# Attention with an image prompt: the Gram sum in 9 matmuls a group, its last one behind the product with V

## The chip, the cores and the metric

The kernel runs on one core of a Trainium2 chip. The metric is the device time of one execution in microseconds: 407.49 as the median of three runs (407.61, 407.49 and 405.20).

## The reference

For each of 8 batches there are 112 queries of 320 channels (20 heads of 16) and a context of 375 tokens of 512 channels, the last 4 of which are an image prompt. Besides the ordinary attention over the 371 text tokens, each head needs the norm of the probability-weighted mean of the raw context.

```python
scores_t = einsum('bhsd,bhtd->bhst', q, k_t) * attn_scale
probs_t  = softmax(scores_t)
text_out = einsum('bhst,bhtd->bhsd', probs_t, v_t)
qsem = l2norm(einsum('bhst,bte->bhse', probs_t, text_ehs))
sem  = einsum('bhse,bne->bhsn', qsem, l2norm(ip_ehs))
fused = einsum(q, k_ip) * attn_scale + 0.5 * sem
probs_ip = softmax(fused) * spatial_mask
out = (text_out + probs_ip @ v_ip) @ W_out + b_out + hidden_states
```

## The kernel before

**The Gram form.** The norm of qsem is not formed from its 512 channels. With G = X X^T over the tokens (371 x 371) and e the exponentials of one head and query, the squared norm is e^T G e. G is cut into three row blocks of 128, 128 and 115 tokens. Only the blocks on and above the diagonal are kept; those above it are counted twice (scale 2.0 in lines 683 and 824). Each block is held as two fp32r parts: Gh is rounded by ACT, Gl is the remainder, made by DVE from the same PSUM bank.

**Units and the order.** `master_schedule` writes out one order of units by hand; every engine walks through it and does its part of each unit, so the order is that of TensorE, and a wait on any engine holds what stands behind it there. `behind` changes the order for DVE alone. A batch has five groups of four heads (words in ROUNDS, one string a group; EARLY is batch 0, SECOND the first group of batch 1, LATE the last group of batches 5 and 6, LAST batch 7). While the groups of batch b run, the units of batch b+1 and the K units of batch b+2 are woven in. The words are:

- St (S0, S1, S2): scores of the next group for a third of the tokens, four matmuls; ACT makes the exponentials `big` (line 703) and a rounded copy `er` (line 707).
- gram (g2, g1, g0, or g for all three): Y = sum over the blocks i up to j of G(i,j)^T e(i), 6, 4 and 2 matmuls of 448 columns (lines 1070 to 1074). DVE multiplies Y by e(j) (line 852), POOL adds the three products (line 565). Y has two PSUM banks, so g0 waits for the product of g2.
- v (pv): the product with V for the group before, and the sums, into O; ACT copies O to OT (line 715).
- G0, G1, G2: the row blocks of G of the next batch, 12 matmuls each of 376, 248 and 120 columns. K0, K1, K2 and V0, V1, V2: the keys and values. m (max): a plain score matmul of one head of the next batch, whose row maximum DVE takes (line 830); there are 20 in a batch. mT: the transpose of the maxima, whose result goes by DMA to qst.
- T0, T1: transposes of OT (line 1105), copied by ACT to R (line 722); r0, r1, r2, pw, z and p are the small steps on POOL, DVE and ACT that make the image-prompt probabilities; pT transposes these (line 1110), cT and o make the output.
- E, El: the rounding split of the context of a batch, by ACT (line 652) and by DVE (line 770, batches 0 and 1) or POOL (line 570).

**The ring.** The units K, G, V, T, pT, cT, o, max and mT take three PSUM banks PR in strict turn: a unit waits until the unit three places before it in the ring has been read out (`freed`). The queries' and keys' terms go through DRAM: ks is written to kd and loaded into kst by DMAs of SP (lines 443 and 376).

In the prologue the order is: split of batch 0, queries, K of batch 0, image-prompt keys and values, split of batch 1, G of batch 0, K of batch 1, then the three V of batch 0 and the qip units spread among the 20 max units of batch 0, mT, G of batch 1, St of group 0 with K0 of batch 2.

## Time and profile before

| what | value |
|---|---|
| runs | 407.61, 407.49, 405.20 us, median 407.49 |
| profiled execution | 406.79 us, of it the span 404.6 us |
| PE busy | 391.4 us (97%), 3680 matmuls |
| PEld busy | 323.8 us (80%) |
| DVE, ACT, POOL busy | 223.1 (55%), 205.2 (51%), 208.1 us (51%) |
| chain that ended last | 86% PE; Y 26%, PR 42%, P 9%, O 8% |
| Gram matmuls | 480, in two groups of 95.3 and 87.3 us busy |
| DMA | 38.03 MB, mean 94 GB/s |

PE is TensorE's matmuls and PEld its weight loads, which run beside them. A record of a matmul is longer than the time until the next one may start, so busy times of PE overlap; the steps between starts tell the cost. In the trace all matmuls have the line of a helper, 947, and the PSUM tile tells them apart: Y is the Gram, P the scores, O the product with V, PR the ring. In brackets behind a row stands how long the engine was idle before it and what ended that.

### The profile page before, as it was taken

The numbers are of one execution on the slowest core, as the hardware profiler recorded it, in microseconds if no ns is written. First come the engines' busy times: TensorE is split into PE (matmuls) and PEld (weight loads), VectorE is DVE, ScalarE is ACT, GpSimd is POOL, SyncE is SP. The second block draws the span as 40 slices with busy tenths as digits, with TensorE's granted clock in tenths as the row PEclk, the third lists the DMA queues.
The fourth block names the chain that finished last, engine by engine and source line by source line (L and its number), as shares of the span: only waits on it lengthen the run. The fifth ranks groups of instructions, "written<-read, shape, count | busy, mean of one in ns | idle before, by whom it ended". The sixth has DMA issues, their size and how long they took to land.

```text
span 404.6 us, 9573 instructions
## 1 busy us (share of the span) xinstructions
PE 391.4 (97%) x3680; PEld 323.8 (80%) x3680; DVE 223.1 (55%) x502; ACT 205.2 (51%) x486; POOL 208.1 (51%) x220
## 2 busy tenths in 40 slices
PE   8999998999999999999999999999999999999985
PEld 6548888778788888888889888888888878886763
DVE  0798363675466535665465636653476547644433
ACT  1434234564646564546456554556454466457822
POOL 3020271282537772586437652787258433935972
PEclk9999999999999999999999999999999999999999
DMA  8499986347204802372217420470208110000000
GB/s 268 125 285 235 217 162 127 102 150 135 70 2 151 147 13 73 107 154 39 83 36 187 75 69 17 151 147 16 72 15 181 29 40 2 2 14 30 2 16 15
DMA packets 29455, 38.03 MB, mean 94 GB/s; under 512 B 14361, under 2 KB 26745, under 8 KB 28729
## 3 DMA queue, kind: packets, MB, share of 16 engines
q1 hardware_dynamic: 28514, 36.36, 37.4%
q10 hardware_dynamic: 896, 1.07, 0.8%
q8 instruction: 29, 0.48, 0.5%
q14 instruction: 16, 0.13, 0.1%
HBM read 28.50 MB, written 8.81 MB: 92 GB/s over the span
## 4 chain that ended last, share of the span: by engine, by line
PE 86%; DMA 3%; ACT 3%; issue 2%; DVE 2%; POOL 2%; SPq 1%; ACTq 0%; DVEq 0%; POOLq 0%
PE PR L947 42%; PE Y L947 26%; PE P L947 9%; PE O L947 8%; DMA et<-ctxT 2%; PE PR L1105 1%; ACT big L703 1%; POOL el L570 1%; ACT er L707 1%; DMA qst<-ma 1%; POOL pb L565 1%; DVE el L770 0%; SPq L474 0%; SPq L395 0%; DVE pb L852 0%
## 5 line engine op out<-in xcount | busy, mean ns | idle before, releaser
L565 POOL TENSOR_TENSOR pb<-pb 128x448 f32<-128x448 f32 x78 | 89.2, 1144 | 100.7 <-DVE pb L852 95.2
L830 DVE TENSOR_REDUCE mx<-PR 112x1 f32<-112x371 f32 x160 | 83.9, 540 | 79.2 <-PE PR L947 78.0
L947 PE MATMUL Y<-er,Gh 128*128 128x448 f32 x240 | 95.3, 397 | 1.9 <-ACT er L707 1.0
L852 DVE TENSOR_TENSOR pb<-big,Y 128x448 f32<-128x448 f32 x120 | 72.7, 621 | 36.3 <-PE Y L947 36.2
L947 PE MATMUL Y<-er,Gl 128*128 128x448 f32 x240 | 87.3, 364 | 0.0
L703 ACT ACTIVATE big<-P 128x448 f32<-128x448 f32 x120 | 65.1, 543 | 17.4 <-PE P L947 16.7
L707 ACT ACTIVATE er<-big 128x448 fp32r<-128x448 f32 x120 | 69.4, 578 | 3.8
L947 PEld LDWEIGHTS Y<-er,Gh 128*128 128x128 f32 x240 | 45.1, 188 | 13.5 <-DVE pb L852 8.2
L947 PE MATMUL PR<-kst,qst 96*112 96x371 bf16 x160 | 51.0, 330 | 0.9 <-DVEq L806 0.8
L947 PEld LDWEIGHTS Y<-er,Gl 128*128 128x128 f32 x240 | 45.2, 188 | 2.1
L947 PE MATMUL P<-qst,kst 99*128 99x112 bf16 x480 | 42.0, 214 | 0.9 <-DMA qst<-ma 0.9
L947 PEld LDWEIGHTS P<-qst,kst 99*128 99x128 bf16 x480 | 29.8, 99 | 15.1 <-issue 7.8
L671 ACT ACTIVATE ks<-PR 128x372 bf16<-128x372 f32 (+1 forms) x24 | 10.3, 429 | 50.7 <-PE PR L947 50.2
L947 PE MATMUL PR<-wvh,eh 128*128 128x320 f32 (+1 forms) x96 | 32.3, 336 | 0.4 <-ACT Vt L695 0.4
L947 PE MATMUL O<-big,Vt 128*22 128x112 f32 x960 | 31.0, 262 | 0.0
L695 ACT ACTIVATE Vt<-PR 128x320 f32<-128x320 f32 (+1 forms) x24 | 10.6, 442 | 39.2 <-PE PR L947 39.2
L947 PE MATMUL PR<-eh 128*128 128x376 f32 (+2 forms) x96 | 29.8, 310 | 0.0
L947 PE MATMUL PR<-wvl,eh 128*128 128x320 f32 (+1 forms) x96 | 29.7, 309 | 0.0
L947 PE MATMUL PR<-wvh,el 128*128 128x320 f32 (+1 forms) x96 | 29.6, 309 | 0.0
L587 POOL TENSOR_TENSOR t<-ssq,halfm 112x20 f32<-112x20 f32 (+2 forms) x9 | 28.8, 3200 | 0.5 <-DVE ssq L868 0.4
L947 PE MATMUL PR<-eh,el 128*128 128x376 f32 (+2 forms) x96 | 28.0, 292 | 0.0
L947 PE MATMUL PR<-el,eh 128*128 128x376 f32 (+2 forms) x96 | 28.0, 292 | 0.0
(171 smaller groups left out, 675.4 us busy)
## 6 DMA issues: line engine op xcount, KB each, us to landing
et<-ctxT SPq DMA_DIRECT2D x8, 752.0 KB, 4.3
kst<-kd SPq DMA_DIRECT2D x7, 720.0 KB, 8.0
kd<-ks SPq DMA_DIRECT2D x16, 288.0 KB, 3.0
qst<-qd SPq DMA_DIRECT2D x48, 70.0 KB, 2.5
kst<-kd SPq DMA_DIRECT2D x7, 480.0 KB, 9.7
kst<-kd SPq DMA_DIRECT2D x9, 240.0 KB, 8.7
qd<-kst SPq DMA_DIRECT2D x4, 336.0 KB, 5.5
vx<-xr SPq DMA_DIRECT2D x8, 140.0 KB, 2.2
```

The lines of the kernel that those rows point to most:

```text
L565: pool.tensor_tensor(total, total, (pz, pm)[j], ALU.add).then_inc(s_S, 1)
L570: pool.tensor_tensor(el[b % 2][:, sl, :], et[:, sl, :], eh[b % 2][:, sl, :].bitcast(f32), ALU.subtract).then_inc(s_el, 1)
L587: power = pool.tensor_tensor(t1[:, hs], ssq[:, hs], halfm[:, hs], ALU.pow)
L671: act.activation(ks[:, 0, TP * c:TP * c + w], bank[:, 0:w], ACT.Copy).then_inc(s_kh, 1)
L695: act.activation(Vt[b % 2][0:r, i, :, 0:D], bank[0:r, 0:C].rearrange("p (h d) -> p h d", d=D), ACT.Copy).then_inc(s_free[seq[u] % NR], 1)
L703: act.activation(e, P[(3 * g + c) % 2][:, 0:448], ACT.Exp).then_inc(s_exp, 1)
L707: act.activation(er[g % 2][:, 448 * c:448 * c + 448], e, ACT.Copy).then_inc(s_er, 1)
L830: dve.tensor_reduce(mx[b % 2][:, h:h + 1], bank[0:S, 0:T], AX.X, ALU.max).then_inc(s_free[seq[u] % NR], 1)
L852: dve.tensor_tensor((pz, pm, pa[g % 2])[j], eb[g % 3][:, 448 * j:448 * j + 448], Y[y % 2][:, 0:448], ALU.mult).then_inc(s_P, 1)
L947: return pe.matmul(o, st, mv, start=start, stop=stop, **kw)
L1105: last = pe.transpose(bank[0:S, 128 * (r - lo):128 * (r - lo) + 128], OT[b % 2][:, r, :], ident[:, :])
```

## The change

The diagonal blocks of G lose their second matmul. A diagonal block is now made so that one fp32r matrix carries all of it: DVE reads the diagonal c out of the bank (a product with the identity, summed into `gc`), limits it from below, takes its reciprocal `grc`, divides the block by c row by row, keeps the part above the diagonal rounded with 0.5 on the diagonal (`half_upper`), and computes the remainder above the diagonal in fp32, `dj`. A new unit D (D0, D1, D2) transposes dj on TensorE and DVE adds it, scaled, to the lower triangle of the same matrix. e is multiplied by c as it is rounded to `er` (scale in the ACT instruction), and the sum is taken twice, by 2.0 instead of 1.0 in `usel`. Off the diagonal Gh and Gl remain, each divided by c. `ident` becomes a third of `masks`, which are loaded at the front of SP's queue.

The order is rewritten: in the groups of batches 0 to 6 g0 is split off and stands behind the product with V (behind S1 in the first group); T0 and T1 move to the second group; the G units and K2 move to other groups; in the prologue G of batch 0 stands ahead of the split of batch 1, V(0,0) ahead of K of batch 1, and only G(1,0) and G(1,1) stay there, with two max of batch 1. `behind` puts Gl behind the second product of the next Gram and the third G block behind mT, and `late_g` puts ACT's part of a G block behind the next St.

```diff
@@ -19,10 +19,12 @@
 GOFF = (0, 384, 640)
+LOFF = (0, 256)
+TINY = 1e-30
 
 STACK = ((0, 3), (1, 2), (2, 1))
-FILLS = 17
-FIRST, REST = 2, 6
+FILLS = 19
+FIRST, REST = 1, 6
@@ -48,18 +50,18 @@
 
-ROUNDS = ("S0 K0 m g m K1 S1 m v S2 m G0 m",
-          "S0 m g m K2 m S1 v m S2 G1 m",
-          "S0 m g2 T0 T1 g1 g0 m r0 G2 m S1 m pw v S2 m V0",
-          "Kr S0 r1 m g m V1 m S1 m m v r2 S2 mT z V2",
-          "p E g2 g1 pT g0 cT S0 S1 v o S2")
-SECOND = "K0 S0 m g m K1 S1 m v S2 m G0 m"
-EARLY = ("m m S0 m g m K1 S1 m S2 K2 m",
-         "S0 m g m S1 m S2 v m m wo",
-         "S0 m g m S1 m v S2 V0 m",
-         "Kr S0 m g m V1 m S1 m m v S2 mT V2",
-         "E g S0 v S1 S2")
-LATE = "p g2 g1 pT g0 cT S0 S1 v S2 o"
+ROUNDS = ("S0 K0 m m g2 g1 m S1 v g0 m m S2 m K1 m G0",
+          "S0 g2 g1 m S1 v g0 T0 T1 r0 m S2 D0 m K2 m V0 m",
+          "S0 g2 g1 m S1 v g0 m pw S2 V1 m G1 m",
+          "Kr S0 r1 g2 g1 m S1 v g0 m D1 r2 S2 m m G2 mT z V2",
+          "p E g2 g1 pT g0 cT S0 S1 v D2 o S2")
+SECOND = "K0 S0 m m g2 g1 m S1 v g0 m m S2 m K1 m G0"
+EARLY = ("S0 m g2 g1 m K1 S1 g0 m S2 K2 m",
+         "S0 m g2 g1 m S1 v g0 m S2 G2 D0 m m wo",
+         "S0 m g2 g1 m S1 v g0 m D1 S2 V0 m m",
+         "Kr S0 g2 g1 m D2 V1 S1 m v g0 m S2 m mT V2",
+         "E g2 g1 g0 S0 v S1 S2")
+LATE = "p g2 g1 pT g0 cT S0 S1 v D2 S2 o"
@@ -81,16 +83,17 @@
     order = [("w", 0)] + split(0) + qs[0]
-    order += [("K", 0, c) for c in range(3)] + [("Kr", 0), ("w", 1)] + qs[1] + [("kip", c) for c in range(3)] + [("vip",)] + split(1)
-    order += [("G", 0, i) for i in range(3)] + [("K", 1, c) for c in range(3)] + [("Kr", 1)]
-    side = [("V", 0, 0), ("V", 0, 1), ("V", 0, 2)] + [("qip", b) for b in range(B)]
+    order += [("K", 0, c) for c in range(3)] + [("Kr", 0), ("w", 1)] + qs[1] + [("kip", c) for c in range(3)] + [("vip",), ("G", 0, 0), ("G", 0, 1)]
+    order += split(1) + [("G", 0, 2), ("V", 0, 0)]
+    order += [u for c in range(3) for u in (("K", 1, c), ("D", 0, c))] + [("Kr", 1)]
+    side = [("V", 0, 1), ("V", 0, 2)] + [("qip", b) for b in range(B)]
     side = spread(side, [("max", 0, h) for h in range(H)])
     cut = side.index(("qip", 3))
     order += side[:cut] + split(2) + side[cut:]
-    order += [("mT", 0)] + [("G", 1, i) for i in range(3)] + [("St", 0, 0), ("St", 0, 1), ("K", 2, 0), ("St", 0, 2)]
+    order += [("mT", 0), ("G", 1, 0), ("K", 2, 0), ("max", 1, 0), ("max", 1, 1), ("St", 0, 0), ("St", 0, 1), ("G", 1, 1), ("St", 0, 2)]
     for b in range(B):
         n, f = b + 1, b - 1
-        maxes = iter([("max", n, h) for h in range(H)])
+        maxes = iter([("max", n, h) for h in range(0 if b else 2, H)])
...
@@ -136,18 +141,41 @@
 
+    out, held, low, last = [], [], [], []
+    for u in order:
+        if u[0] == "K" and u[1] >= 2:
+            out, held = out + held, [u]
+        elif u[0] == "G" and u[1] < 2:
+            out, held = out + held + [u], [("Gl",) + u[1:]] if u[2] < 2 else []
+        elif u[0] == "G" and u[2] < 2:
+            out, low = out + low + [u], [("Gl",) + u[1:]]
+        elif u[0] == "G":
+            last.append(u)
+        else:
+            out.append(u)
+            if u[0] in ("max", "gram", "mT", "o", "K"):
+                out, held = out + held, []
+            if u[0] == "gram" and u[2] == 1:
+                out, low = out + low, []
+            if u[0] == "mT":
+                out, last = out + last, []
+    return out + held
+
+
+def late_g(order):
+
     out, held = [], []
     for u in order:
-        if u[0] in ("K", "G") and u[1] >= 2:
-            out, held = out + held, [u]
+        if u[0] == "G" and u[1] >= 2 and u[2] < 2:
+            held.append(u)
         else:
             out.append(u)
-            if u[0] in ("max", "gram", "mT", "o"):
+            if u[0] == "St":
                 out, held = out + held, []
     return out + held
 
 
-RING = ("K", "G", "V", "T", "pT", "cT", "o", "max", "mT")
+RING = ("K", "G", "D", "V", "T", "pT", "cT", "o", "max", "mT")
...
@@ -231,6 +262,7 @@
         vrTh, vrTl = [w[:, 0, 0:H * NIP * 3].rearrange("p (c n) -> p c n", c=3) for w in (eh[0], el[0])]
+        ident, half_upper, upper = [masks[:, 128 * i:128 * i + 128] for i in range(3)]
...
@@ -399,9 +434,10 @@
             load_x(1)
+            sp.dma_start(masks[:, :], ident_d).then_inc(s_mk, 16)
             ip = [(ET_IP[:, :, :], ctxip), (hq[:, :, :], hm_q), (wkip_s, wkip.rearrange("(c p) n -> p c n", p=128)),
                   (wvip_s, wvip.rearrange("(c p) n -> p c n", p=128))]
-            first = [(kst[0][96:99, :, :], krow.rearrange("r (h t) -> r h t", h=H)), (ident[:, :], ident_d)]
+            first = [(kst[0][96:99, :, :], krow.rearrange("r (h t) -> r h t", h=H))]
@@ -517,7 +553,9 @@
             fill(usel[:, :], 0.0)
-            fill(usel[:, 21:22], 1.0)
+            fill(usel[:, 21:22], 2.0)
+            for i in range(2):
+                fill(gc[i][:, :], 1.0)
@@ -630,7 +668,7 @@
             act.dma_start(wv_s, wv.rearrange("(c p) n -> p c n", p=128)).then_inc(s_wr_, 16)
-            for u in order:
+            for u in late_g(order):
@@ -671,17 +709,18 @@
                     b, i, r = u[1], u[2], ROWS[u[2]]
-                    filled(act, u)
+                    if i < 2:
+                        act.wait_ge(s_gd, 2 * b + i + 1)
+                    else:
+                        filled(act, u)
                     if b == 0:
                         act.wait_ge(s_set, FILLS)
                     if b >= 2:
                         act.wait_ge(s_gram, 3 * NG * (b - 1))
-                    a = min(128, T - 128 * i)
-                    act.activation(Gh[b % 2][0:r, GOFF[i]:GOFF[i] + a], bank[0:r, 0:a], ACT.Copy)
-                    rest = T - 128 * i - a
+                    rest = T - 128 * i - r
                     if rest:
-                        act.activation(Gh[b % 2][0:r, GOFF[i] + a:GOFF[i] + a + rest], bank[0:r, a:a + rest],
-                                              ACT.Copy, scale=2.0)
+                        act.activation(Gh[b % 2][0:r, GOFF[i] + r:GOFF[i] + r + rest], bank[0:r, r:r + rest],
+                                       ACT.Copy, scale=grc[b % 2][0:r, i:i + 1])
@@ -704,7 +743,8 @@
                         act.wait_ge(s_gram, 3 * (g - 1))
-                    act.activation(er[g % 2][:, 448 * c:448 * c + 448], e, ACT.Copy).then_inc(s_er, 1)
+                    act.activation(er[g % 2][:, 448 * c:448 * c + 448], e, ACT.Copy,
+                                   scale=gc[g // NG % 2][:, c:c + 1]).then_inc(s_er, 1)
@@ -814,16 +854,39 @@
                         dve.wait_ge(s_set, FILLS)
+                        dve.wait_ge(s_mk, 16)
+                    if b >= 2:
+                        dve.wait_ge(s_gram, 3 * NG * (b - 1))
+                    filled(dve, u)
+                    if i == 2:
+                        dve.wait_ge(s_gh, 3 * b + 3)
+                    c, rc = gc[b % 2][0:r, i:i + 1], grc[b % 2][0:r, i:i + 1]
+                    low, diag = dj[i][0:r, 0:r], Gh[b % 2][0:r, GOFF[i]:GOFF[i] + r]
+                    link(dve.scalar_tensor_tensor(low, bank[0:r, 0:r], 1.0, ident[0:r, 0:r], ALU.mult, ALU.mult, accum_out=c))
+                    link(dve.tensor_scalar(c, c, TINY, None, ALU.max))
+                    link(dve.reciprocal(rc, c))
+                    link(dve.scalar_tensor_tensor(diag, bank[0:r, 0:r], rc, half_upper[0:r, 0:r], ALU.mult, ALU.mult))
+                    dve.scalar_tensor_tensor(low, bank[0:r, 0:r], rc, diag.bitcast(f32), ALU.mult,
+                                             ALU.subtract).then_inc(s_gd if i < 2 else s_free[seq[u] % NR], 1)
+                    if i < 2:
+                        dve.wait_ge(s_gd, 2 * b + i + 1)
+                    else:
+                        freed(dve, seq[u])
+                    dve.scalar_tensor_tensor(low, low, c, upper[0:r, 0:r], ALU.mult, ALU.mult).then_inc(s_ru, 1)
+                elif k == "Gl":
+                    b, i, r = u[1], u[2], ROWS[u[2]]
+                    n = seq[("G", b, i)]
+                    o, rest = GOFF[i], T - 128 * i - r
                     dve.wait_ge(s_gh, 3 * b + i + 1)
-                    gh, gl = Gh[b % 2], Gl[b % 2]
-                    a = min(128, T - 128 * i)
-                    rest = T - 128 * i - a
-                    o = GOFF[i]
-                    low = dve.tensor_tensor(gl[0:r, o:o + a], bank[0:r, 0:a], gh[0:r, o:o + a].bitcast(f32), ALU.subtract)
-                    if rest:
-                        low = dve.scalar_tensor_tensor(gl[0:r, o + a:o + a + rest], bank[0:r, a:a + rest], 2.0,
-                                                       gh[0:r, o + a:o + a + rest].bitcast(f32), ALU.mult, ALU.subtract)
-                    low.then_inc(s_free[seq[u] % NR], 1)
+                    dve.scalar_tensor_tensor(Gl[b % 2][0:r, LOFF[i]:LOFF[i] + rest], PR[n % NR][0:r, r:r + rest],
+                                             grc[b % 2][0:r, i:i + 1], Gh[b % 2][0:r, o + r:o + r + rest].bitcast(f32),
+                                             ALU.mult, ALU.subtract).then_inc(s_free[n % NR], 1)
+                elif k == "D":
+                    b, i, r = u[1], u[2], ROWS[u[2]]
+                    filled(dve, u)
+                    diag = Gh[b % 2][0:r, GOFF[i]:GOFF[i] + r]
+                    dve.scalar_tensor_tensor(diag, bank[0:r, 0:r], grc[b % 2][0:r, i:i + 1], diag.bitcast(f32), ALU.mult,
+                                             ALU.add).then_inc(s_free[seq[u] % NR], 1)
@@ -1017,6 +1080,12 @@
                     last.then_inc(s_ring, 1)
+                elif k == "D":
+                    b, i, r = u[1], u[2], ROWS[u[2]]
+                    pe.wait_ge(s_ru, 3 * b + i + 1)
+                    if b == 0 and i == 0:
+                        pe.wait_ge(s_mk, 16)
+                    pe.transpose(bank[0:r, 0:r], dj[i][0:r, 0:r], ident[0:r, 0:r]).then_inc(s_ring, 1)
...
@@ -1063,15 +1133,18 @@
                     if j == 2 and r == 0:
-                        freed(pe, seq[("G", b, 2)])
+                        for i in range(3):
+                            freed(pe, seq[("D", b, i)])
                     if j == 2:
                         pe.wait_ge(s_er, 3 * g + 3)
                     d = Y[y % 2][:, 0:448]
                     for i in range(j + 1):
                         o = GOFF[i] + 128 * (j - i)
                         mv = er[g % 2][:, 448 * i:448 * i + 448]
-                        mm(d, Gh[b % 2][:, o:o + 128], mv, i == 0, False)
-                        last = mm(d, Gl[b % 2][:, o:o + 128], mv, False, i == j)
+                        last = mm(d, Gh[b % 2][:, o:o + 128], mv, i == 0, i == j)
+                        if i < j:
+                            o = LOFF[i] + 128 * (j - i - 1)
+                            mm(d, Gl[b % 2][:, o:o + 128], mv, False, False)
...
```

## Rows read from the trace of the kernel before

**Rows 1.** stretches: length, busy us (instructions) of PE, PEld, DVE, ACT, POOL; granted clock; DMA share; GB/s
```profile
240.50:284.50 44.00, 43.99 (x442) 37.88 (x441) 24.43 (x55) 24.15 (x58) 25.79 (x25) 1.00 0.37 89
365.00:405.00 40.00, 32.53 (x371) 24.27 (x371) 16.43 (x49) 19.00 (x49) 24.86 (x31) 0.98 0.05 16
```

**Rows 2.** waits of weight loads, 196.6 to 240.5: total us, times, longest
```profile
PEld Y L947 <- DVE pb L852: 1.0, 4, 0.3
```

**Rows 3.** order of time, weight loads of one Gram: start us, us, engine, operation
```profile
251.14 0.19 PEld L947 LDWEIGHTS Y<-er,Gl 128*128 128x128 f32 x1
251.61 0.19 PEld L947 LDWEIGHTS Y<-er,Gh 128*128 128x128 f32 x1 [0.28 <-DVE pb L852]
...
251.92 0.13 PEld L947 LDWEIGHTS PR<-kst,qst 96*112 96x112 bf16 x1
```

**Rows 4.** groups of instructions, whole span: busy us, mean ns, idle before
```profile
L947 PE MATMUL Y<-er,Gl 128*128 128x448 f32 x240 | 87.3, 364 | 0.0
```

**Rows 5.** chain that ended last, in the last batch: start us, us, what
```profile
371.01 0.88 POOL vx L578
...
378.77 0.90 PE O L947 x32
```

**Rows 6.** order of time: transposes of the sums and ACT's copies of them
```profile
258.53 0.66 PEld L1105 LDWEIGHTS PR<-ident,OT 128*112 128x112 f32 x5
...
259.36 0.77 ACT L722 ACTIVATE R<-PR 112x512 f32<-112x512 f32 x2 [0.55 <-PE PR L1105]
```

**Rows 7.** groups of instructions of DVE, whole span
```profile
L830 DVE TENSOR_REDUCE mx<-PR 112x1 f32<-112x371 f32 x160 | 83.9, 540 | 79.2 <-PE PR L947 78.0
L852 DVE TENSOR_TENSOR pb<-big,Y 128x448 f32<-128x448 f32 x120 | 72.7, 621 | 36.3 <-PE Y L947 36.2
...
L822 DVE TENSOR_TENSOR Gl<-PR,Gh 128x128 fp32r<-128x128 f32 x16 | 4.6, 286 | 2.4 <-ACT Vt L687 2.4
...
L883 DVE RECIPROCAL zm<-zm 112x8 f32<-112x8 f32 x1 | 0.2, 203 | 0.0
```

**Rows 8.** order of time, DVE: the last reduces and two linked operations of mT
```profile
270.70 1.45 DVE L830 TENSOR_REDUCE mx<-PR 112x1 f32<-112x371 f32 x3 [1.01 <-PE PR L947]
...
272.73 0.26 DVE L837 TENSOR_SCALAR ma<-PR 20x112 bf16<-20x112 f32 x1 [0.44 <-PE PR L1042]
273.03 0.26 DVE L838 SCALAR_TENSOR_TENSOR mr<-PR,ma 20x112 f32<-20x112 f32 x1
```

**Rows 9.** order of time, TensorE: one St and the max behind it
```profile
249.18 0.36 PE L947 MATMUL P<-qst,kst 99*128 99x112 bf16 x4
249.38 0.32 PE L947 MATMUL PR<-kst,qst 96*112 96x371 bf16 x1
```

**Rows 10.** order of time, from mT's load to pT's load
```profile
272.39 0.09 PEld L1042 LDWEIGHTS PR<-ident,mx 112*20 112x20 f32 x1
...
274.16 0.19 PEld L947 LDWEIGHTS Y<-er,Gh 128*128 128x128 f32 x1
...
275.01 0.33 POOL L601 TENSOR_TENSOR pe_<-pe_,zm 112x80 f32<-112x80 f32 x1
...
276.12 0.12 PEld L1110 LDWEIGHTS PR<-ident,pe_ 112*80 112x80 f32 x1
```

**Rows 11.** order of time in the prologue, several engines
```profile
34.01 0.44 PE L947 MATMUL PR<-eh 128*128 128x376 f32 x1
...
36.45 1.79 DVE L770 TENSOR_TENSOR el<-et,eh 128x752 fp32r<-128x752 f32 x2 [0.56 <-ACT eh L652]
...
38.81 0.44 PE L947 MATMUL PR<-eh,wkh 128*128 128x372 f32 x1
...
53.55 1.25 SPq L376 DMA_DIRECT2D kst<-kd  x3
...
67.80 0.55 PE L947 MATMUL P<-qst,kst 99*128 99x112 bf16 x8 [0.49 <-DMA qst<-ma]
```

**Rows 12.** a stretch, columns as in rows 1
```profile
66.00:68.00 2.00, 1.51 (x19) 1.41 (x18) 0.82 (x4) 0.96 (x5) 0.00 (x0) 1.00 0.06 17
```

More of the change, by code:

```diff
@@ L100, in master_schedule @@
                 unit.update({"V0": ("V", n, 0), "V1": ("V", n, 1), "V2": ("V", n, 2), "mT": ("mT", n)})
-            if b and n < B:
+            if n < B:
                 unit.update({"G0": ("G", n, 0), "G1": ("G", n, 1), "G2": ("G", n, 2)})
+            if n < B:
+                unit.update({"D0": ("D", n, 0), "D1": ("D", n, 1), "D2": ("D", n, 2)})
             if n + 1 < B:
@@ L194, in build @@
         Gh = [sb(f"Gh{i}", [128, 768], f32r) for i in range(2)]
-        Gl = [sb(f"Gl{i}", [128, 768], f32r) for i in range(2)]
+        Gl = [sb(f"Gl{i}", [128, 384], f32r) for i in range(2)]
+        gc = [sb(f"gc{i}", [128, 3]) for i in range(2)]
+        grc = [sb(f"grc{i}", [128, 3]) for i in range(2)]
+        dj = [sb(f"dj{i}", [128, 128]) for i in range(3)]
         Vt = [sb(f"Vt{i}", [128, 3, H, MV]) for i in range(2)]
@@ L208, in build @@
         mask_s = sb("mask_s", [S, 1])
-        ident = sb("ident", [128, 128])
+        masks = sb("masks", [128, 3 * 128])
         ones = sb("ones", [128, S])
@@ L264, in build @@
         s_w2 = sem("s_w2")
+        s_mk = sem("s_mk")
         s_pw = sem("s_pw")
@@ L295, in build @@
         s_pad = sem("s_pad")
+        s_gd = sem("s_gd")
         s_gh = sem("s_gh")
+        s_ru = sem("s_ru")
         s_ms = sem("s_ms")
@@ L1040, in _ @@
                         pe.wait_ge(s_w, 16 * FIRST)
+                        pe.wait_ge(s_mk, 16)
                     freed(pe, seq[("max", b, H - 1)])
@@ L1213 @@
         "bout": np.ascontiguousarray(L0_xattn_b_out),
-        "ident_d": np.eye(128, dtype=np.float32),
+        "ident_d": np.concatenate([np.eye(128), np.triu(np.ones((128, 128)), 1) + np.eye(128) / 2,
+                                   np.triu(np.ones((128, 128)), 1)], 1).astype(np.float32),
         "hm_q": np.ascontiguousarray(hm_q),
```

## The prediction

> **What bounds the kernel now.** I read the stretches first, then the waits of TensorE, then the chain. In one full batch (240.5 to 284.5 us) TensorE is busy for 43.99 of 44.00 us at the full granted clock, DVE for 24.4, ACT for 24.2 and POOL for 25.8 [rows 1]: TensorE's issue order is the time, and a matmul less is a gain only if nothing else becomes late. What TensorE loses to others in a batch is little: 1.0 us in 4 waits for the product on DVE that frees a Gram bank [rows 2]. The reader should see in the loads how such a wait looks: the one at 251.61 comes late, the one two further (251.92) is 0.78 us behind 251.14 where three steps of 0.20 would be 0.60, so each wait costs 0.18 us net [rows 3]. The step of 0.20 us is the price of one Gram matmul; its record lasts 0.364 us [rows 4], so a result is ready about 0.2 us after the engine went on (0.16, and 0.04 for the semaphore).
>
> **Removed.** Three of 12 Gram matmuls in each of 40 groups: 120 x 0.20 = -24.0 us. The last one (g0) now stands behind the product with V, 0.90 us long [rows 5], so the Y bank is free when it comes: 4 x 0.18 = 0.7 us a batch in batches 0 to 6, -5.0 us. ACT loses one Gh copy per block; not on the path.
>
> **Added on TensorE.** Three transposes a batch. Five transposes are issued in 0.66 us [rows 6], so 0.13 each, 24 x 0.13 = +3.1 us. If nothing waited, the total would be 406.8 - 24.0 - 5.0 + 3.1 = 381.
>
> **Added on DVE.** Each G block now has a chain in which every instruction waits for the one before. It isn't in the trace; I bound it by rows. Three are 128x128 operations from PSUM (0.286 us each), two are on 128x1 (the nearest is a reciprocal of 112x8, 0.203 us) [rows 7]; a linked successor starts 0.30 us after a 0.26 us one, so 0.04 between [rows 8]. Three x 0.286 + 2 x 0.20 + 4 x 0.04 = 1.4 us up to the release of ACT, and 0.25 for the rounding remainder behind it: 1.65 us, with ends of 1.2 (short operations at 0.1) and 1.9. Behind its waits stand on DVE the next reduces and the Gram products, on ACT (which waits for the chain before it copies Gh) the exponentials of the next St, and behind any wait of TensorE the whole rest of its order. Together with the add after the transpose DVE gets some 5 us more a batch, 29.5 of about 44: it does not become the bound by its sum, but four places in a batch become waits of TensorE, because ring banks (three of them, in strict order) come free through DVE. In each I count from one point what TensorE issues (max 0.17, estimated from 371 of 448 columns of 0.20; St 0.20 [rows 9]; pv 0.90; transposes 0.13) and what DVE has to do. The three reduces in 1.45 us [rows 8] show that two that follow each other overlap by some 0.08.
> - A, first group of a batch: K1 needs the bank of the max behind g0. From g0's issue TensorE has three max and one St, 0.71; DVE has 0.20 + product 0.62 + reduce 0.54 - 0.08 + 0.05 = 1.33. Wait 0.65.
> - B, second group: K2 needs the bank of the max that stands behind T0 T1, and on DVE the reciprocal r0 stands before that max and waits for ACT's copy of R, which ends 1.60 us after the first transpose load [rows 6]. 1.60 + 0.25 + 0.54 = 2.4 against 0.66 + 2 max + St + D0 = 1.33 on TensorE. Wait 1.0.
> - C, fourth group: from the end of G1, TensorE issues four max, three St, nine Gram matmuls, pv and D1 in 4.1 us; DVE, 0.20 + chain 1.6, then four reduces, three products and Gl, about 5.25, before max m20 may start. Wait 1.15.
> - D, fifth group: the chain of G2 was put right behind mT, ahead of the two operations of p. Before, mT's load was at 272.39, POOL's p ended at 275.34, pT was loaded at 276.12 [rows 10]: 0.78 of slack. The chain adds 1.6 and the Gram is 0.4 shorter by then: 1.6 + 0.4 - 0.78 = 1.2; I take 1.1.
> The sum is 3.9 us a batch, against 3.0 + 0.7 - 0.4 = 3.3 gained. In the six batches 1 to 6: +23.4 us. Ends: 2.4 a batch (chain 1.2, B at half) and 5.
>
> On the first operation of the chain, which also sums: the rows show no such instruction, and I took it at 0.286. The Trainium skill, VectorE: DVE Perf Modes, in the section on two Vector instructions with no wait between them, says that an operation that writes its accumulator is two instructions. By that C and D would each grow by one short instruction, 0.1 to 0.2 us by the rows of short ones [rows 7]: 12 x 0.2 = 2.4 us, 415. No row here bears it out yet.
>
> **The start.** Now the G blocks of batch 0 come before the split of batch 1. G(0,0) starts at 34.01 and takes some 2.15 of the 4.8 us that its three blocks take until K(1,0) at 38.81 [rows 11]. DVE: chain 36.35 to 38.0, wait for ACT's two copies and Gl to 38.85, chain of G(0,1) to 40.2; ACT can only then copy, and split batch 1 (before: done on DVE at 36.45 + 1.79 = 38.24). The split ends at about 43.2. With V(0,0) (1.77, as from mT's load to the next Gram's [rows 10]) put before it, it would be at 40.65. It waits for 43.4: 2.75 us. K(1,2) is then 4.9 us later; so is the load of kst for batch 1, issued at 53.55 and over by about 66, where the transfers fall to a share of 0.06 [rows 12]. The first max of batch 1 now stands ahead of St(0,0), which began at 67.80 [rows 11]: it waits until about 71. Behind it ACT waits for the chain of G(1,1) before it can do the exponentials of the last St of group 0, some 0.9 us more. I come to the first Gram 4.9 us later than before, of which 0.4 are transposes; the G block moved out of this stretch and the two max moved in make 0.8: waits of 5.3 us. The masks (192 KB for 64 KB) are now loaded early; cover is that they are issued behind ctxT, and if they delayed anything it would be by 1 us at most.
>
> **Batch 0.** G(1,2) now stands two ring places ahead of a max; its chain waits for ACT's copy, and DVE frees the bank some 1.9 us after TensorE left it, while TensorE has 0.3 to issue: 1.6. From mT to the next batch's first St a DMA has the word, so 0.6 of that group's gain is not realised. +2.2.
>
> **Batch 7.** No K, G, V or max are left to hide ACT and POOL (19.0 and 24.9 us busy in the last 40 [rows 1]); POOL's vx and t stand between sums there [rows 5]. One of the 3.0 us is lost: +1.0.
>
> **Sum.** -24.0 - 5.0 + 3.1 + 23.4 + 5.3 + 2.2 + 1.0 = +6.0 on 406.8 (the profiled execution, span 404.6, 0.7 below the median of 407.5): 413.
>
> **Elsewhere.** er is scaled by a tile instead of by nothing: same instruction, 0. ACT's wait for the G chain is put behind St, where ACT is busy until about the same moment: 0; without that cover it would be up to 0.4 us three times a batch. K2 leaves 3 us later in its batch than before, with its copy on POOL, its DMAs on SP and the kst load behind; about 8 us of slack remain until the next batch's max: 0.
>
> **The rivals.**
> 1. The chain is half as long (0.8 us): C falls to 0.3, D to 0.3, the start loses 2 and batch 0 one: 413 - 6 x 1.65 - 3 = 400, faster. This is the one on the other side; it decides at a chain of about 1.2, where C and D still cost 0.7 each and the batch is even. For it: several short rows overlap. Against: each link here is a semaphore, and the linked rows show 0.04 between them and no overlap.
> 2. Nothing waits: TensorE stays packed and the time is 381 to 386. For it: DVE has 19 us idle in a batch. Against: the four places above, which are orders in the code and not averages.
> 3. A and B cost half (ACT's copies come earlier): 413 - 6 x 0.8 = 408, no change to be measured.
> 4. The waits grow (weight loads exposed behind each, 0.1 x 24, the accumulator, the start): 420.
>
> **How the numbers follow.** My case 0.48, rival 1 0.22, rival 2 0.08, rival 3 0.16, rival 4 0.06. A run tells no change within 1% (403.4 to 411.6). Faster: rivals 1 and 2, 0.30. Same: rival 3 and the low end of mine, 0.24. Slower: 0.46. The range must reach rival 1 with its own spread, and half of 4: 396 to 420; my case alone is 408 to 418.
>
> **What would show it.** 360 Gram matmuls at a step of 0.20; in a full batch, waits of TensorE's loads for a reduce (K1, K2, m20) of 2.5 to 3 us and for POOL's p of 1.1; batch period 44 to 45 us; chain 1.4 us to the release; K(1,0) at 43.4. I am wrong if the period is under 42.5, or if the chain on DVE takes under 1.2 us.

## The result

The changed kernel takes 425.74 us (median of 4 runs, 424.95 to 426.49), the kernel before 406.74 beside it: a ratio of 1.047 (95% interval 1.043 to 1.051), slower. The forecast was 413, with 420 as the upper end. The profiled execution took 425.68 us, its span is 423.9 for 404.6: +19.3 us.

The stretches, one full batch and the last 40 us (columns as in [rows 1]):

```profile
252.00:297.18 45.18, 42.39 (x430) 36.13 (x429) 29.11 (x76) 25.39 (x56) 25.72 (x26) 1.00 0.37 86
384.00:424.00 40.00, 31.26 (x364) 22.19 (x363) 16.68 (x49) 21.00 (x52) 24.77 (x31) 0.95 0.05 15
```

TensorE, packed in [rows 1], now idles 2.8 us of a batch of 45.18. DVE grew from 24.4 to 29.1 and is far from full. These are all the weight loads of the batch that waited over 0.3 us (in brackets the idle time before each and what released it):

```profile
260.89 0.19 PEld L1010 LDWEIGHTS PR<-eh,wkh 128*128 128x128 f32 x1 [0.73 <-DVE mx L893]
270.11 0.14 PEld L1088 LDWEIGHTS PR<-masks,dj 128*128 128x128 f32 x1 [0.37 <-ACT R L762]
270.99 1.14 PEld L1010 LDWEIGHTS PR<-et,wk 128*64 128x64 f32 x16 [0.59 <-DVE mx L893]
285.72 0.13 PEld L1010 LDWEIGHTS PR<-kst,qst 96*112 96x112 bf16 x1 [0.36 <-DVE Gl L881]
287.15 0.13 PEld L1010 LDWEIGHTS PR<-kst,qst 96*112 96x112 bf16 x1 [0.84 <-DVE mx L893]
293.15 0.12 PEld L1183 LDWEIGHTS PR<-masks,pe_ 112*80 112x80 f32 x1 [1.20 <-issue]
293.85 0.30 PEld L1010 LDWEIGHTS PR<-masks,tn 112*128 112x128 f32 x2 [0.48 <-issue]
```

These are the places A to D of the prediction: A (0.73), B (0.37 and 0.59), C (0.36 and 0.84) and D (1.20 and 0.48). The "issue" at 293.15 is pT, which waits for POOL's p; of the 0.48 behind it 0.30 stood there before. The waits of [rows 2] for the Y bank are gone. The chain on DVE (start, duration; compare [rows 7, 8]):

```profile
265.55 0.29 DVE L865 SCALAR_TENSOR_TENSOR dj<-PR,masks 128x128 f32<-128x128 f32 x1 [1.15 <-PE PR L1010]
265.76 0.08 DVE L865 DVE_READ_ACCUMULATOR dj<-PR,masks 128x1 f32 x1
265.88 0.15 DVE L866 TENSOR_SCALAR gc<-gc 128x1 f32<-128x1 f32 x1
266.07 0.16 DVE L867 RECIPROCAL grc<-gc 128x1 f32<-128x1 f32 x1
266.27 0.35 DVE L868 SCALAR_TENSOR_TENSOR Gh<-PR,grc,masks 128x128 fp32r<-128x128 f32 x1
266.65 0.35 DVE L869 SCALAR_TENSOR_TENSOR dj<-PR,grc,Gh 128x128 f32<-128x128 f32 x1
267.04 0.35 DVE L875 SCALAR_TENSOR_TENSOR dj<-dj,gc,masks 128x128 f32<-128x128 f32 x1
```

It takes 1.45 us to the end of L869, which releases ACT, and 1.84 in all: 1.4 and 1.65 were forecast.

The next table says where the 19.3 us arose, by marks of TensorE's loads. The forecast's column is its terms sorted by the same marks. A fifth group stands behind mT: it saves 0.6 (in batch 0 nothing, by the forecast) and from batch 1 on holds one D of 1.1. The column's sum is 6.1 by rounding.

| stretch | before | after | difference | forecast |
|---|---|---|---|---|
| to the first Gram | 72.14 | 79.95 | +7.8 | +4.9 |
| from there to mT of batch 1 | 26.67 | 30.49 | +3.8 | -0.3 |
| mT of batch 1 to mT of batch 7 | 256.31 | 263.90 | +7.6 | +3.0 |
| from there to the end | 49.48 | 49.56 | +0.1 | -1.5 |

A full batch went from 44.02 to 45.18. All kernels below are told by this period (from one mT to the next, batches 3 to 5) and by the start of the first Gram. The second number is less exact than the first: G(0,0), up to which the code of some kernels is the same, began at 32.8 to 34.8 in four kernels with the start of before and at 33.0 to 36.3 in eight with the changed start.

### The profile page after: what moved, and what is told of

The parts are those of the page before. It is cut to its first block, busy times and chain, and to the rows that moved or that the text cites. A ratio compares the mean times of both kernels' runs of the same rounds, so it can differ in the third digit from the quotient of the medians.

```text
span 423.9 us, 9580 instructions
## 1 busy us (share of the span) xinstructions
PE 383.3 (90%) x3584; PEld 312.0 (74%) x3584; DVE 262.5 (62%) x670; ACT 214.5 (51%) x462; POOL 207.0 (49%) x222
## 3 DMA queue, kind: packets, MB, share of 16 engines
q10 hardware_dynamic: 896, 1.07, 0.9%
## 4 chain that ended last, share of the span: by engine, by line
PE 62%; DVE 17%; POOL 6%; issue 6%; ACT 4%; DMA 3%; SPq 1%; DVEq 0%; ACTq 0%; POOLq 0%
PE PR L1010 34%; PE Y L1010 14%; PE P L1010 7%; PE O L1010 5%; DVE pb L915 3%; DVE mx L893 3%; DMA qst<-qd 2%; DVE Gh L868 1%; DVE dj L869 1%; POOL t L625 1%; POOL pb L603 1%; ACT big L742 1%; DVE dj L865 1%; POOL el L608 1%; DVE dj L875 1%
## 5 line engine op out<-in xcount | busy, mean ns | idle before, releaser
L893 DVE TENSOR_REDUCE mx<-PR 112x1 f32<-112x371 f32 x160 | 82.9, 536 | 42.4 <-PE PR L1010 41.1
L1010 PE MATMUL Y<-er,Gh 128*128 128x448 f32 x240 | 89.6, 399 | 4.7 <-ACT er L746 3.6
L915 DVE TENSOR_TENSOR pb<-big,Y 128x448 f32<-128x448 f32 x120 | 71.2, 613 | 29.4 <-PE Y L1010 28.6
L746 ACT ACTIVATE er<-big,gc 128x448 fp32r<-128x448 f32 x120 | 80.4, 670 | 3.9
L1010 PE MATMUL PR<-kst,qst 96*112 96x371 bf16 x160 | 49.6, 333 | 8.0 <-DVE mx L893 4.4
L1010 PEld LDWEIGHTS Y<-er,Gh 128*128 128x128 f32 x240 | 45.6, 190 | 14.7 <-issue 4.8
L1010 PE MATMUL Y<-er,Gl 128*128 128x448 f32 x120 | 44.4, 370 | 0.0
L1010 PEld LDWEIGHTS P<-qst,kst 99*128 99x128 bf16 x480 | 31.8, 99 | 13.8 <-issue 4.9
L1010 PEld LDWEIGHTS PR<-kst,qst 96*112 96x112 bf16 x160 | 19.8, 129 | 16.2 <-DVE mx L893 6.3
L1010 PE MATMUL PR<-eh,wkh 128*128 128x372 f32 x64 | 23.4, 366 | 5.3 <-DVE Gl L881 2.7
```

The lines of the kernel that those rows point to most:

```text
L746: act.activation(er[g % 2][:, 448 * c:448 * c + 448], e, ACT.Copy, scale=gc[g // NG % 2][:, c:c + 1]).then_inc(s_er, 1)
L893: dve.tensor_reduce(mx[b % 2][:, h:h + 1], bank[0:S, 0:T], AX.X, ALU.max).then_inc(s_free[seq[u] % NR], 1)
L915: dve.tensor_tensor((pz, pm, pa[g % 2])[j], eb[g % 3][:, 448 * j:448 * j + 448], Y[y % 2][:, 0:448], ALU.mult).then_inc(s_P, 1)
L1010: return pe.matmul(o, st, mv, start=start, stop=stop, **kw)
```

## The experiments

| kernel | median us | ratio | first Gram | period |
|---|---|---|---|---|
| 9 matmuls alone | 392.72 | 0.963 (0.959 to 0.967) | 72.56 | 42.2 |
| g0 late alone | 406.34 | 0.996 (0.994 to 0.998) | 73.21 | 43.9 |
| 9 matmuls and g0 late | 388.76 | 0.953 (0.945 to 0.961) | 70.52 | 41.5 |
| new order, no chain | 401.72 | 0.989 (0.981 to 0.996) | 73.55 | 42.9 |
| chain without its first three steps | 412.06 | 1.011 (1.003 to 1.019) | 75.78 | 44.1 |
| changed, start as before | 424.76 | 1.041 (1.038 to 1.045) | 77.84 | 45.2 |
| changed, p first | 420.73 | 1.032 (1.023 to 1.041) | 80.87 | 44.3 |
| changed, no scale on er | 425.11 | 1.042 (1.037 to 1.046) | 81.08 | 45.2 |

**9 matmuls alone.**

```diff
-                        mm(d, Gh[b % 2][:, o:o + 128], mv, i == 0, False)
-                        last = mm(d, Gl[b % 2][:, o:o + 128], mv, False, i == j)
+                        last = mm(d, Gh[b % 2][:, o:o + 128], mv, i == 0, i == j)
+                        if i < j:
+                            mm(d, Gl[b % 2][:, o:o + 128], mv, False, False)
```

> The kernel before without the three products of the low part of the diagonal blocks with er (9 matmuls per group; that part of the result is left out); order, banks and everything on ACT, DVE and POOL as before. Theory: a Gram matmul is worth its step of 0.20 us, 120 x 0.20 = -24; but between g2 and g0, which share a Y bank, TensorE now has 0.2 us less to issue, so each wait for the product on DVE grows by 0.2 where nothing else stands between: about 30 x 0.2 = +6. 407 - 18 = 389 (386 to 393). Rival: something that the profile of before hides (ACT's St to er path, the reduces) becomes late as soon as TensorE is 2.4 us a batch faster: 396 to 402.

The edit gives a diagonal block only the matmul with its Gh. Measured: -15.2 us. The Y waits grew more than expected, by 1.16 us a batch; g0 of the second group, 0.28 late in [rows 3], is now

```profile
244.77 0.19 PEld L947 LDWEIGHTS Y<-er,Gh 128*128 128x128 f32 x1 [0.64 <-DVE pb L852]
```

So 15 x 0.20 = 3.0 are saved, 1.16 given back: 44.02 to 42.2.

**g0 late alone** (`g` becomes `g2 g1` with g0 behind v).

> The kernel before with g0 moved behind the product with V in the groups 1 to 4 of batches 1 to 6, still 12 matmuls. By the prediction's price the 24 waits for the Y bank go, 24 x 0.18 = -4.3: 402.5. Rival: the two matmuls that now stand between others of another shape begin with an exposed load (0.31 us for one in the trace of the changed kernel, for 0.20), +0.11 x 24 = +2.6, so 405 and no difference that can be seen.

Measured: -0.14 a batch, 0.4% in all; the rival. The idle 0.18 in front of the split g0 is no loss: in the kernel before the unit behind v idled as long.

```profile
246.54 0.21 PEld L947 LDWEIGHTS P<-qst,kst 99*128 99x128 bf16 x4 [0.18 <-ACT big L703]
```

What the split costs is the step: from g0's load (246.71) to the next unit's (247.22) it is 0.51 us for 2 x 0.20, so 0.11 each time. Besides, pT now waits 0.26 us for POOL's p.

**Both** (the two edits together).

> The kernel before with 9 matmuls per group and g0 behind the product with V, nothing else: no chain, no transposes, no scale (the low part of the diagonal blocks is left out of the result). It shows what the first two items of the change are worth together. The kernel with 9 matmuls alone has a period of 42.21 with Y waits of 0.68 + 0.64 + 0.48 in the groups that are split here; the split costs 4 x 0.18 for an exposed load: 42.21 - 1.80 + 0.72 = 41.1, x 7 gives 392.7 - 7.6 = 385 (383 to 388). Rival (the two items gain nothing together, another wait comes): 390 to 393.

Measured: 388.76, the fastest of all; 41.5 a batch, 0.4 over the theory. Now pT waits for POOL's p without any chain:

```profile
221.60 0.12 PEld L1111 LDWEIGHTS PR<-ident,pe_ 112*80 112x80 f32 x1 [0.68 <-issue]
222.31 0.30 PEld L947 LDWEIGHTS PR<-ident,tn 112*128 112x128 f32 x2 [0.48 <-issue]
```

It is the place of g0 in the fourth group that makes p late. The sum of its product stands on POOL ahead of z, and p ends 3.9 us behind mT's load both here and with g0 late alone, but 2.9 behind it in the kernel before and with 9 matmuls alone, where pT does not wait. The gain of the change's first two items is 2.5 us a batch, not the 3.7 of the forecast: four split g0 at 0.11 and this wait (0.68, and 0.48 for 0.30) make up the difference.

**New order, no chain** (the D units, the DVE part of G and both scales removed; ACT rounds the whole block again, and the low part of the diagonal is left out).

> The changed kernel in its new order and with 9 matmuls, but without the chain on DVE, the transposes D and both scales: Gh as in the kernel before on ACT, no low part of the diagonal (left out of the result). Theory (the chain is the loss): waits C 1.2 and D 1.2 and the transposes 0.4 go in each batch, 2.8 x 7 = -20, and about 5 us of the start: 400 (397 to 404). Rival (the order alone is the loss; A and B, the split g0, the late split of batch 1): 412 to 420.

Measured: 401.72, near the theory. The order alone costs 1.4 a batch over the kernel with both items: A is 0.73, B 0.38 and C 0.83 without any chain, while pT does not wait. In the place of C this is

```profile
267.74 0.17 PEld L983 LDWEIGHTS PR<-eh 128*115 128x115 f32 x1 [0.83 <-DVE mx L866]
```

a wait for the reduce behind the product with g0, as in A. Chain, D and scale cost 2.25 more a batch, 6.4 up to the first Gram (1.8 of these stand ahead of G(0,0), 34.85 for 33.02, where there is no chain yet) and 4.1 between mT of batch 0 and of batch 1.

**The start as before.**

```diff
-    order += [..., ("vip",), ("G", 0, 0), ("G", 0, 1)]
-    order += split(1) + [("G", 0, 2), ("V", 0, 0)]
+    order += [..., ("vip",)] + split(1)
+    order += [("G", 0, i) for i in range(3)]
```

> The changed kernel with one part undone: the prologue up to the first max of batch 0 in the order of before (the split of batch 1 ahead of the three G blocks, the first V block back behind them). Theory: the wait of K(1,0) (2.65 us) and the halved clock behind it (about 1.4 us) go: -4 to -5, 421. Rival: with the chains then ahead of K(1,0)'s copies on ACT and DVE the wait only moves: 424 to 426.

Measured: no difference worth the name in the median (424.76), the rival. The wait moved: K(1,0) waits 0.88 us and K(1,1) 1.19 for banks that the chains hold. The first Gram came 2.1 us earlier; a stretch of lower clock (0.80 and 0.85 in the 10 us from 155) took 1.5 back in this execution.

**p ahead of the chain of G2 on DVE** (`last` flushed at p, not at mT).

> The changed kernel with one place undone: on DVE the two operations of p stand ahead of the chain of G2 again. In the changed kernel p's reduce starts at 291.69, behind a chain that began at 290.00, and pT is loaded at 293.15, 1.20 us late, the transposes behind it another 0.48. Theory (the place is the loss): p ends 1.4 us earlier on POOL, TensorE is done with its Gram at 291.95, the bank of pT is released at about 291.9: D goes down to 0.2 and each of six batches is 1.2 to 1.5 us shorter, period 43.8, 417 (416 to 419). Rival (DVE is late as a whole in this place, and the chain only comes behind another waiter, the product with g2): period 44.8, 423.

Measured: -0.88 a batch, -5 us in all, between theory and rival. D's 1.68 went, and a wait of 0.66 for the product with g2, now behind the chain, came for it. So D is the chain's place on DVE, at 0.88 a batch where 1.2 to 1.5 were expected.

**A and B by order.** In the first group `v m g0 m` for `v g0 m m`, in the second `g2 T0 T1 g1 ... v m g0`.

> The changed kernel with a new order in two groups of each batch: in the first one the max whose bank K1 needs stands ahead of g0, in the second the transposes T0 T1 stand behind g2 (as in the kernel before) and a max ahead of g0. Theory: the waits A (0.73) and B (0.37 + 0.59) go, 1.7 us a batch in six batches, -10: period 43.5, 415.5 (414 to 418). Rival (DVE is too full, a wait that goes here comes back at the next bank): period 44.7 to 45.2, 422 to 426.

Measured: 427.72 us (ratio 1.047, 1.037 to 1.057), period 44.9. A is gone; B came back larger, since the max behind T0 T1 now follows three places after G0 and meets a bank that the chain, ACT's copy and Gl still hold:

```profile
270.08 0.13 PEld L1010 LDWEIGHTS PR<-kst,qst 96*112 96x112 bf16 x1 [1.47 <-DVE Gl L881]
```

**A shorter chain.**

```diff
-                    link(dve.scalar_tensor_tensor(low, bank[0:r, 0:r], 1.0, ident[0:r, 0:r], ALU.mult, ALU.mult, accum_out=c))
-                    link(dve.tensor_scalar(c, c, TINY, None, ALU.max))
-                    link(dve.reciprocal(rc, c))
```

> The changed kernel with gc and grc preset to 1 by POOL and without the three instructions that work them out (sum, max, reciprocal; the scaling is left out): the chain ahead of ACT's release is 0.75 us for 1.46. This is rival 1 of the prediction, made real. Theory: C falls by 0.6 and D by 0.7 in each of six batches, the start by 1.5 to 2, batch 0 by 0.7: period 43.9, 415 (413 to 418). Rival (the chain's length is not what counts, the order is): period 44.8, 422.

The three operations that work out the diagonal and its reciprocal are removed; c and its reciprocal are preset to 1, so the scaling is left out of the result. Measured: 412.06, -13.7 us for three operations of 0.7 us a block. Of it 1.07 a batch: D falls from 1.68 to 0.97, and C's 0.36 goes, but not its 0.84:

```profile
276.25 0.13 PEld L1008 LDWEIGHTS PR<-kst,qst 96*112 96x112 bf16 x1 [0.78 <-DVE mx L891]
```

The first Gram is 4.2 earlier (1.4 of it already ahead of G(0,0)) and batch 0 3.0 shorter, and this execution's clock never halved on the way. The last two numbers mix the chain's length with the clock, and no run parts them. Rival 1 of the prediction, made real, is not faster than the kernel before.

**No scale on er** (the scaling by c is left out of the result).

> The changed kernel without the scale tile on er (ACT's copy as before; the scaling by gc is left out of the result). Its copies took 670 ns in the changed kernel for 578 before, 120 x 0.09 = 11 us of ACT. Theory (none of it is on the path in a full batch, some in the last one and at the first Gram): period 45.2, 0 to -1.5 in all, 424 to 426. Rival (ACT's path from St to er holds TensorE): 3 to 4 us less.

Measured: nothing in a full batch. The term "same instruction, 0" was right for the time, although the copy takes 670 ns for 578.

**The clock.** In the changed kernel K(1,0) takes the bank of G(0,1), and its Gl stands on DVE behind the split of batch 1:

```profile
44.27 0.33 DVE L881 SCALAR_TENSOR_TENSOR Gl<-PR,grc,Gh 128x115 fp32r<-128x115 f32 x1
```

TensorE, ready at 42, waits 2.65 us for it and then works at half clock, 1.2 GHz. Columns: stretch, us, PE busy, granted clock, DMA:

```profile
42.00:44.00 2.00, 0.00 (x0) 1.00 1.08 165
44.00:46.00 2.00, 1.34 (x4) 0.63 0.36 61
46.00:48.00 2.00, 2.00 (x8) 0.52 0.00 0
```

> The changed kernel with 16 matmuls of 320 columns into a free bank put ahead of K(1,0), where TensorE waits 2.65 us for the bank. They take about 2.35 us, so they fit into the wait. In the changed kernel the 12 matmuls of K(1,0) that follow take 3.46 us for 1.99 in K(1,1), at a granted clock of 0.50. Theory (TensorE's own idle time lowers the clock): K(1,0) starts where it did (44.7) and takes 2.0 us, the start is 1.5 us shorter, 424.3. Rival (the clock falls for another reason at that time): K(1,0) still takes about 3.4 us, 425.7.

The edit puts 16 matmuls into a free bank ahead of K(1,0). The same view with the wait filled:

```profile
44.00:46.00 2.00, 1.83 (x13) 1.00 1.25 192
46.00:48.00 2.00, 1.87 (x11) 1.00 0.84 124
```

For this wait the cause is shown: K(1,0) took 1.99 us for 3.46. The total did not move (426.76): this execution's clock was also halved at 32 to 36 us, ahead of G(0,0) and with TensorE busy (as in the changed kernel's at 30 to 35, and in both runs with the start of before and one item of the change; not explained), and twice in batch 0. Nor does every wait of this size lower the clock: the kernel below with the order of before waits 1.62 and 2.15 us in each full batch, and its granted clock stays at 1.00 from 84 to 415 us.

**All the arithmetic in another order.** First the order of before, with the chains in it:

> The whole arithmetic of the changed kernel (9 matmuls, chain, D, both scales) in the order of the kernel before: its prologue, its places of K, T, G and max; g0 behind the product with V, D0 behind g0 of the second group, D1 in the third, D2 in the fourth, each chain on DVE directly behind the next reduce or product. Theory (the chain costs what its places make of it): the kernel with 9 matmuls, g0 late and no chain has a period of 41.5; the transposes add 0.4, and waits for the banks of G0 and G1 about 1: 43.0 a batch, the first Gram at about 76: 401 (397 to 406). Rival (wherever the chain stands, DVE's 5 us more are paid once): period 44.5, 411 or more.

Measured: 426.1 (1.046, 1.042 to 1.050), period 46.4, the rival and worse. G0 and G1 hold a bank through chain, ACT's copy and Gl, and the unit three places on waits:

```profile
263.34 0.13 PEld L1006 LDWEIGHTS PR<-kst,qst 96*112 96x112 bf16 x1 [1.62 <-DVE Gl L877]
272.12 0.52 PEld L1174 LDWEIGHTS PR<-masks,OT 128*112 128x112 f32 x5 [2.15 <-DVE Gl L877]
```

In a full batch the order that the change brought is better for its own chain than the old one; in the total the two are equal.

Then this order with the block copied to SBUF by ACT, so that the bank is free at once. D1 now stands behind g1, and some units of the prologue and of batch 0 moved too:

> The whole arithmetic of the changed kernel in the order of the kernel before, but ACT first copies the sums of a G block from their bank to SBUF and frees the bank at once; chain, scaled copy and low part read the copy. Theory (it is not DVE's work that costs, but that a bank is held through the chain): the waits of the same order with the bank held (1.62 for m, 2.15 for T0, 0.96 for D1, period 46.4) go, the period is 42.2 (41.5 without the chain, 0.4 for D, some tenths for ACT), the first Gram at about 75: 395 (391 to 400). Rival (DVE's and ACT's added work is late anyway): period 44, 408.

Measured: 418.28 (1.030, 1.022 to 1.037), period 44.03 for 46.4. The waits of 1.62 and 2.15 went, and the order around them is the same, so the held bank was their cause; D1 waits 1.67 instead, for a reduce that stands behind a chain. The total missed the theory (395) by far. Operations of the chain that read SBUF also ran into POOL (batch 0):

```profile
90.04 1.62 DVE L871 SCALAR_TENSOR_TENSOR Gh<-gB,grc,masks 115x115 fp32r<-115x115 f32 x1
91.69 0.81 DVE L872 SCALAR_TENSOR_TENSOR gB<-gB,grc,Gh 115x115 f32<-115x115 f32 x1
```

```profile
89.96 1.56 POOL L576 TENSOR_TENSOR wol<-kst,woh 128x640 fp32r<-128x640 f32 x1 [0.49 <-ACT woh L675]
91.48 0.90 POOL L577 TENSOR_TENSOR wol<-kst,woh 64x320 fp32r<-64x320 f32 x1
```

Each of the two DVE operations ends 0.1 us behind POOL's. Better places for the chain:

> As the kernel with the copied blocks, in a better order: D1 behind the product with V of the third group (it waited 1.67 us there in each batch), G2 behind g0 and D2 behind the next product with V; in batch 0 G(1,2) one group later, away from POOL's split of wo, beside which three operations of its chain took 0.79, 1.62 and 0.81 us for 0.28 and 0.35. Theory (with the bank free at once, the chain can be placed so that nothing waits for it): period 44.03 - 1.67 = 42.4, batch 0 2.5 us less: 413.6 - 10 - 2.5 = 401 (398 to 405), faster than the kernel before by 1.3%. Rival (DVE's and POOL's conflict over operands in SBUF moves with the chain): period 43.5, 408 to 410.

Measured: 417.04 (1.026, 1.021 to 1.031), period 44.4, short of both theory and rival. D1's wait went from 1.67 to 0.23, but the max that now stands in its place waits 1.66 for a reduce, which stands on DVE behind the chain of G1. What a chain delays is not only its own bank but the reduce behind it. And that chain meets POOL in every full batch:

```profile
263.08 1.20 POOL L601 TENSOR_TENSOR pb<-pb 128x448 f32<-128x448 f32 x1
263.70 0.73 DVE L871 SCALAR_TENSOR_TENSOR Gh<-gB,grc,masks 128x128 fp32r<-128x128 f32 x1
264.24 0.92 POOL L614 TENSOR_TENSOR vx<-vx,hv 80x320 f32<-80x320 f32 x1
264.46 0.84 DVE L872 SCALAR_TENSOR_TENSOR gB<-gB,grc,Gh 128x128 f32<-128x128 f32 x1
```

The two operations take 0.73 and 0.84 us for 0.35, here and in the kernel with the copy before it. By an estimate from these rows, 0.87 of the 1.66 is this meeting and not the chain's own length; no run parts the two.

Last, the changed kernel with p first and one max ahead of g0 in two groups:

> The changed kernel with p ahead of the chain of G2 on DVE, and in the first two groups one max moved ahead of g0 (T0 T1 stay where the change put them). Theory (the waits are additive where their places are far apart): 44.3 as with p alone, less 0.73 for A, less 0.4 for B: 43.2, and 425.7 - 5 - 7 = 413 (411 to 417). Rival (B only moves to the max behind D0, whose bank ACT frees late): 43.6, 416 to 418.

Measured: 416.07 (1.021, 1.015 to 1.027), period 43.2 as the theory had it; the total is 3 us above it, and batch 0 took 45.6 us for 41.9, at half clock in two stretches (78 to 86 and 94 to 102). Of the kernels with all the arithmetic none is better (the copy in better places is not told apart from it), and it is still slower than before. A kernel that beats both is the one with 9 matmuls and g0 late, 388.76, which leaves the low part of the diagonal blocks out.

## Why the prediction was wrong

The steps that failed are the gain of a batch (forecast 3.7 us, measured 2.5), and the price of the waits in the start and in batch 0, which had one late bank too few and no term for the clock. That the waits A to D came out near their forecast is in part luck, as C shows.

**Right:** the sign; that waits would come at the four places in a batch; the chain's length; that DVE would not be the bound by its sum; the 0 for er. The waits listed above sum to 4.6 in a batch, for 3.9. **Right in size, wrong in cause:** C was worked out as 1.15 us from the chain of G1, and rival 1 let it fall to 0.3 with a shorter one. It measured 0.36 and 0.84, and the 0.84 stays at 0.78 with half the chain and at 0.83 with none: it belongs to the order, a reduce behind the product with g0, and the chain's share is the 0.36. B, worked out without the chain at 1.0, is 0.38 and 0.17 without it and 0.37 and 0.59 with it.

**The gain of a batch**, -3.0 - 0.7, failed: it is -2.5. Four split g0 cost 0.11 more than their step (0.4 for a forecast 0), and g0 behind v in the fourth group makes POOL's p late (0.9 for a forecast 0). In the new order without the chain pT does not wait, so D in the changed kernel is the chain's. The waits as a term were then worth 1.4 (order, less the wait of pT that it removes) + 1.85 (chain, without the 0.4 of the transposes) = 3.3 for a forecast 3.9, so the period missed by 0.6 only: 44.02 - 2.5 + 3.3 + 0.4 = 45.2.

**Batch 0**, "+2.2", -0.3 up to the mark with its gains, is the largest miss of a single batch: +3.8. The bank of G(1,2) was late by 1.86 for a forecast 1.6, but a second bank in a row, the one that D frees on DVE, was late too, and the clock was halved behind them (loads of two max of batch 1, then the stretches as above):

```profile
93.92 0.13 PEld L1010 LDWEIGHTS PR<-kst,qst 96*112 96x112 bf16 x1 [1.86 <-DVE dj L869]
95.37 0.13 PEld L1010 LDWEIGHTS PR<-kst,qst 96*112 96x112 bf16 x1 [1.05 <-DVE Gh L888]
```

```profile
92.00:94.00 2.00, 0.43 (x4) 1.00 0.88 258
94.00:96.00 2.00, 1.11 (x8) 0.93 0.12 24
96.00:98.00 2.00, 2.00 (x7) 0.50 0.55 131
98.00:100.00 2.00, 2.00 (x39) 0.72 1.22 192
```

The changed kernel without the scale and the one with the filled wait, whose order here is the same, took 44.9 and 43.6 from mT of batch 0 to that of batch 1 for 41.9: this cost varies by 3 us between executions. Both had a stretch more at half clock, at 80 to 86 us, right behind the wait for the first Gram.

**The start**, +4.9, came to +7.8. K(1,0) was 1.3 later than worked out, of which 0.84 stand ahead of G(0,0) (34.85 for 34.01) and are not the change's; the rest is there because its bank waits for a Gl behind the split, where the forecast had the split alone. Its 12 matmuls took 1.5 more. The wait for the exponentials of group 0 behind the chain of G(1,1), forecast as 0.9 more, is the longest of the start:

```profile
79.98 0.45 PE L1010 MATMUL Y<-er,Gh 128*128 128x448 f32 x1 [2.72 <-ACT er L746]
```

Its load idles 2.93 here and 1.07 in the new order without the chain. That the clock can fall was in no term. [rows 1] show 1.00 in the full batch, and the forecast waits of 2 us and more were priced at their length only.

**The end**, -1.5, came to +0.1. With p first the stretch takes 48.2 and with both items alone 48.1, for 49.6: what this stretch gains is 1.4 and not the 2.6 of that forecast without D, and the D wait in it takes it all.

The accumulator's read, left out of the sum, is 0.08 us a block (the line at 265.76); the Trainium skill, VectorE: DVE Perf Modes, in the section on two Vector instructions with no wait between them, has it right as an instruction of its own, and 415 for 413 would have been as wrong.

## What to carry to other kernels

Matmuls saved between two users of one bank are partly given back as a longer wait for that bank; time the saving alone before paying for it with other work. A serial chain on an engine that frees banks in order costs twice, through the bank that it holds and through the releases queued behind it; copying the operand out removed the first part only, and made the chain longer where it met POOL. A wait that comes out at the forecast size can have another cause: the run without the suspected cause tells. Where a wait of 2 us or more is introduced, look at the granted clock behind it: the time lost there can come on top, though it does not always.

## What the runs showed of the hardware

- A wait of 2.65 us of TensorE in the start was followed by a granted clock of about 0.5, the level of 1.2 GHz (12 matmuls in 3.46 us for 1.99); filled with matmuls it was not. Waits of 1.62 and 2.15 us in each full batch of the kernel with the order of before were not (1.00 from 84 to 415 us). Nor was K(1,0)'s wait of 1.94 us with the shorter chain.
- From mT of batch 0 to that of batch 1 the executions of six kernels with the same order there took 41.9 to 45.6 us; the longer ones show more time at the lower level.
- On DVE a 128x128 operation with a scalar from a tile took 0.35 us for 0.286 without; ACT's 128x448 copy with a scale from a tile took 670 ns for 578.
- DVE operations with both tensors in SBUF took 0.73 to 1.62 us beside POOL's for 0.35, each until about 0.1 us after POOL's ended. The Trainium skill, SBUF — State Buffer, in the section on its two separate sides, says that DVE with two inputs in SBUF and a GpSimd operation that reads SBUF exclude each other for a whole instruction. The trace agrees, and the chain's L868 and L869 from PSUM stayed at 0.35 throughout.
